# Maxima of two heads per instruction, and three PSUM banks instead of four behind ScalarE

## The chip, the cores and the metric

The kernel runs on one core of a Trainium2 chip. The metric is the device time of one execution in microseconds (us). Five engines work side by side, each with its own queue in program order: PE (TensorE, the matmuls), DVE (VectorE), ACT (ScalarE), POOL (GpSimd) and SP (SyncE, which issues DMAs). They meet only at semaphores. Matmuls write to PSUM, which has eight banks of 128 x 512 floats; another engine has to empty a bank before PE may write it again.

## The reference

For 8 sequences of 1024 tokens of width 256, a layer of attention (16 heads of width 16, rotary positions on the last 256 tokens) and a mixture of experts behind it. Cut to what matters here:

```
x = x + attention(layernorm(x))        # this change is in here
    q, k, v = xn @ wq + bq, xn @ wk, xn @ wv + bv      # 8 sequences, 16 heads, 1024 tokens, width 16
    scores = q @ k.T / 4                               # per head 1024 x 1024
    out = softmax(scores) @ v                          # softmax subtracts the row's maximum
    attention = out @ wo + bo
x = x + experts(layernorm(x))          # 16 experts, top 128 tokens each, and a shared one
```

## The kernel before

Attention works in 512 steps, 64 for each of the 8 sequences. A step V takes one group of four heads, one half of the queries (512) and one of eight tiles of 128 keys. Eight steps make a unit (one group, one half of the queries).

Scores are computed twice. **Row scores** (`score_rows`, L928): 128 queries by 512 keys of one head into one of three banks `ring`; DVE takes the row maximum of each bank (`maximum`, L630), joins the two halves of the keys once in a unit (`join_halves`, L636), and POOL writes the maxima beside the queries, so that later scores come with the maximum subtracted. The maxima run 12 steps ahead (`LEAD`), so there are twelve leading steps with nothing but row scores and a few value projections. **Turned scores** (`score_turned`, L939): 128 keys by 512 queries of one head into one of the banks `rot`; ACT takes the exponential of each (`empty`, L770). **Values** (`weigh_values`, L950): two steps later PE multiplies the exponentials with the values; all four heads of a unit add up in the bank `pv`, which ACT copies to `OT` once in a unit (`evacuate`, L824).

PE's order within a step is written out at the end of its block (L956 to L973). In this text a step reads, in PE's order:

- **A**: two row scores (heads 2 and 3); then **T0, T1**: two turned scores
- **PV**: the values of the step two before
- **B**: two row scores (heads 0 and 1); then **T2, T3**: two turned scores
- **side items** (`beside`, L108, by the table `BESIDE`): work of the sequence before or behind, none, one or two of them in a step. Projections q, k, v and the output projection are six matmuls each (L62 to L64); `xt`, `aot`, `x2t` and `ot` are transposes; `lg` are the router's logits. The transposed output `ot` stands in every eighth step (V % 8 == 3), ahead of the table's item.

What T0 to T3 and the side items write goes through the banks `rot` in turn, in PE's order (`ORDER`, L129, and `PLACE`), and ACT empties them in the same order. The item with number n waits until item n - ROT has been emptied (`bank`, L853, `rot_done`). For the row scores, `score_rows` waits in the same way on `ring_done` (L926). PE is one queue: a wait of T1 holds PV, B, T2 and T3 of its step behind it.

In the steps with V % 8 == 1, ACT's copy of `pv` to `OT` stands between the exponentials of T2 and T3 (L838). I call these **OT steps**.

After attention a second block (`feed_forward`, L984) runs the experts; the change does not touch it.

Of the kernel before, what the change touches and what calls it, by code (L numbers as in the profile page):

```python
# [4 lines left out]
F32 = mybir.dt.float32  # L5
# [7 lines left out]
AX = mybir.AxisListType  # L13

P = 128
# [51 lines left out]
def attention(nc, d, ident, SC, B):  # L67
# [9 lines left out]
    UNITS = 2 * G  # L77
    LEAD, LAG = 12, 2
    ROPE_TILES = 2
    ROT = 4  # L80
    RING = 3
    P_STEPS = 3
    LAST = B * STEPS
    CHECKS = 32 * UNITS * B
    TILES = (6, 7, 0, 1, 2, 3, 4, 5)


# [20 lines left out]
    def beside(V):  # L108

        b, S = V // STEPS, V % STEPS  # L110
        out = []
        if V >= 11 and S % 8 == 3:
            unit = (V - 11) // 8
            out.append(("ot", unit // UNITS, unit % UNITS))
        table = BESIDE if V >= 0 else FIRST
        if S in table:
            more, kind, *rest = table[S]
            if 0 <= b + more < B:
                out.append((kind, b + more, *rest))
        return out  # L120
# [16 lines left out]

    def check(m):

        unit, n = m // 32, m % 32  # L140
        return unit, (2, 3, 0, 1)[n % 4], n // 4 % 2, 4 * (unit % 2) + n // 8

    ctx = ExitStack()
    with ctx:
        def sb(name, shape, dt):
            return ctx.enter_context(nc.sbuf_tensor("sb_" + name, shape, dt))

        def sem(name):
            return ctx.enter_context(nc.semaphore(name))
# [21 lines left out]
        QT = [sb(f"QT{g}", [P, T], BF16) for g in range(G)]  # L171
        KT = [sb(f"KT{g}", [P, T], BF16) for g in range(G)]
# [8 lines left out]
        MX = sb("MX", [P, 2, 2, 4, 4], F32)  # L181
# [20 lines left out]
        total = sb("total", [P, TT], F32)  # L202
        act_scratch = sb("act_scratch", [P, 1], F32)

        ring = [ctx.enter_context(nc.psum_tensor(f"ring{i}", [P, 512], F32)) for i in range(RING)]
        rot = [ctx.enter_context(nc.psum_tensor(f"rot{i}", [P, 512], F32)) for i in range(ROT)]
        pv_bank = ctx.enter_context(nc.psum_tensor("pv", [P, 512], F32))

# [24 lines left out]
        ring_full = sem("ring_full")  # L233
        ring_done = sem("ring_done")
# [119 lines left out]
        def _(pool):  # L354
# [51 lines left out]
            def split(item, hi, lo, ready):  # L406

                _, b, h, half = item
                c = slice(512 * half, 512 * half + 512)
                pool.wait_ge(rot_done, done(item))  # L410
                own.inc(nc.gpsimd.tensor_copy(hi[:, h, c], XT[:, h, c]))
                own.wait(pool)
                nc.gpsimd.tensor_tensor(lo[:, h, c], XT[:, h, c], hi[:, h, c].bitcast(F32), ALU.subtract).then_inc(ready, 1)
# [173 lines left out]
        def _(dve):  # L587
# [38 lines left out]
            def maximum(m):  # L626

                unit, j, half, qt = check(m)
                dve.wait_ge(ring_full, m + 1)
                nc.vector.reduce_max(MX[:, unit % 2, half, j, qt % 4:qt % 4 + 1], ring[m % RING][:], AX.X  # L630
                                     ).then_inc(ring_done, 1)

            def join_halves(unit):

                dve.wait_ge(ring_done, 32 * (unit + 1))
                nc.vector.tensor_tensor(MX[:, unit % 2, 0], MX[:, unit % 2, 0], MX[:, unit % 2, 1],  # L636
                                        ALU.max).then_inc(maxima_ready, 1)

            def weighted(unit):

                dve.wait_ge(rot_done, done(("ot", unit // UNITS, unit % UNITS)))
                nc.vector.reciprocal(RD[:], AR[:, :, HD]).then_inc(recip_ready, 1)

            def top_logits(b):

                dve.wait_ge(rot_done, done(("lg", b, 3)))
                if b:
                    dve.wait_ge(shifted_ready, b)
                nc.vector.reduce_max(top[:], LG[:], AX.X).then_inc(top_ready, 1)

            def total_powers(b):

                dve.wait_ge(powers_ready, b + 1)
                if b:
                    dve.wait_ge(scored, b)
                own.inc(nc.vector.reduce_sum(total[:], powers[:], AX.X))
                own.wait(dve)
                nc.vector.reciprocal(total[:], total[:]).then_inc(total_ready, 1)
# [56 lines left out]
            for V in range(-LEAD, LAST):  # L715
                b, S = V // STEPS, V % STEPS
                prev = b > 0
                m = 4 * (V + LEAD)
                if m < CHECKS:
                    maximum(m)  # L720
                    maximum(m + 1)
                if V >= 13 and V % 8 == 5:
                    weighted((V - 13) // 8)
                if m < CHECKS:
                    maximum(m + 2)
                    maximum(m + 3)
                    if m % 32 == 28:
                        join_halves(m // 32)
                if prev and S == 52:
                    top_logits(b - 1)  # L730
                if prev and S == 56:
                    total_powers(b - 1)
# [23 lines left out]
        def _(act):  # L756
# [3 lines left out]
            def empty(item):  # L760

                n = PLACE[item]
                R = rot[n % ROT]
                kind = item[0]
# [85 lines left out]
        def _(pe):  # L850
            pe.wait_ge(ident_in, 16)

            def bank(item):  # L853

                n = PLACE[item]
                if n >= ROT:
                    pe.wait_ge(rot_done, n - ROT + 1)
                return rot[n % ROT]

# [55 lines left out]
            def head(j):  # L915

                return slice(QUAD * j, QUAD * j + QUAD)

            def score_rows(m):

                unit, j, half, qt = check(m)
                b, g = unit // UNITS, unit % UNITS // 2
                if m % 64 == 0:
                    pe.wait_ge(qk_turned[g], 32 * (b + 1))
                if m >= RING:
                    pe.wait_ge(ring_done, m - RING + 1)  # L926
                r = head(j)
                nc.tensor.matmul(ring[m % RING][:], QT[g][r, P * qt:P * qt + P], KT[g][r, 512 * half:512 * half + 512],  # L928
                                 start=True, stop=True, tile_position=(r.start, 0)).then_inc(ring_full, 1)

            def score_turned(V, j):

                unit = V // 8
                b, g, qh, kt = unit // UNITS, unit % UNITS // 2, unit % 2, V % 8
                if kt == 0 and j == 0:
                    pe.wait_ge(q2_turned[unit % 2], 16 * (unit // 2 + 1))
                R = bank(("ex", V, j))
                r = head(j)
                nc.tensor.matmul(R[:], KT[g][r, P * kt:P * kt + P], QT[g][r, 512 * qh:512 * qh + 512], start=True, stop=True,  # L939
                                 tile_position=(r.start, 0)).then_inc(rot_full, 1)  # L940

            def weigh_values(V):

                unit, kt = V // 8, V % 8
                b, g = unit // UNITS, unit % UNITS // 2
                if kt == 0 and unit:
                    pe.wait_ge(ot_ready, unit)
                pe.wait_ge(rot_done, done(("ex", V, 3)))
                for j in range(4):
                    out = nc.tensor.matmul(pv_bank[head(j), :], VA[b % 2][:, kt, 4 * g + j, :], PR[V % P_STEPS][:, j, :],  # L950
                                           start=(kt == 0), stop=(kt == TT - 1))
                out.then_inc(pv_done, 1)
# [1 line left out]
            for item in HEAD:  # L954
                fill(item)
            for V in range(-LEAD, LAST):  # L956
                m = 4 * (V + LEAD)
                if m < CHECKS:
                    score_rows(m)
                    score_rows(m + 1)  # L960
                if V >= 0:
                    for j in range(2):
                        score_turned(V, j)
                if V >= LAG:
                    weigh_values(V - LAG)
                if m < CHECKS:
                    score_rows(m + 2)
                    score_rows(m + 3)
                if V >= 0:
                    for j in range(2, 4):  # L970
                        score_turned(V, j)
                for item in beside(V):
                    fill(item)  # L973
# [596 lines left out]
def program(nc, d, B):  # L1570
    d["xn2T"] = nc.dram_tensor("xn2T", (B * D, 1024), F32, kind="Internal").ap()
    with ExitStack() as ctx:
        SC = ctx.enter_context(nc.sbuf_tensor("gate_scores", [P, 1024 // P, B * E], F32))
        ident = ctx.enter_context(nc.sbuf_tensor("identity", [P, P], F32))
        attention(nc, d, ident, SC, B)
        feed_forward(nc, d, ident, SC, B)
# [28 lines left out]
```

## Time and profile before

| | |
|---|---|
| three runs, us | 2276.67, 2281.63, 2284.34 (median 2281.63) |
| the profiled execution, us | 2277.96 |
| its span, first to last instruction, us | 2276.2 |
| PE busy, us (share of the span) | 2142.0 (94%) |
| DVE busy | 1884.7 (83%) |
| ACT busy | 1619.9 (71%) |
| POOL busy | 1207.2 (53%) |
| 2048 row maxima (L630), busy us | 1279.7 |
| 2048 exponentials (L770), busy us | 1119.5 |
| first and last turned score (L939), us from the start | 75.7 and 1402.1 |

Busy times are unions of the instructions' spans; an instruction of DVE or ACT that follows another closely begins, in the trace, before the other has ended, so that the mean of one is longer than its share of the busy time. The 1.8 us between span and execution lie before the first and behind the last instruction. Attention takes the stretch from the start to some 1430 us, the experts the rest.

### The profile page before, as it was taken

What the parts mean: (1) busy time and instruction counts of PE and PEld (TensorE: products, weight loads), DVE (VectorE), ACT (ScalarE), POOL (GpSimd) and SP (SyncE); (2) the same over time, 40 slices, a digit from 0 to 9 for tenths busy, and PEclk for the clock granted to TensorE, in tenths of its full rate; (3) what the DMA queues carried; (4) which work ended last, traced back from release to release, by engine and by line L of the source; (5) the groups of instructions that cost most, each with busy time, mean ns of one, the idle gap of its engine ahead of it and who ended that gap; (6) DMA issues with size and microseconds to landing.
All of it is one profiled execution on the core that took longest, in us unless ns stands there. A gap on an engine that the chain in (4) does not pass through costs nothing. (4 is left out here: it accounts for less than half of the span.)

```text
span 2276.2 us, 41913 instructions
## 1 busy us (share of the span) xinstructions
PE 2142.0 (94%) x15246; PEld 1232.7 (54%) x15246; DVE 1884.7 (83%) x3135; ACT 1619.9 (71%) x3092; POOL 1207.2 (53%) x1750
## 2 busy tenths in 40 slices
PE   5899999999999999999999988799999999999996
PEld 3233333333333343343343323688888888888886
DVE  6899999999999999999999994587656666666663
ACT  2599999999999999999999997333345455455451
POOL 3434576576576576586582450000024777777773
PEclk8799999999999999999999999899999999999998
DMA  4002013113103113113112111523246667667662
GB/s 118 8 24 36 18 42 73 42 39 71 54 27 81 44 39 79 36 46 70 36 43 55 36 45 40 176 83 111 83 106 144 146 120 151 146 122 149 145 123 35
DMA packets 272425, 173.03 MB, mean 76 GB/s; under 512 B 177664, under 2 KB 253312, under 8 KB 272256
## 3 DMA queue, kind: packets, MB, share of 16 engines
q1 hardware_dynamic: 247680, 137.25, 23.1%
q0 software_dynamic: 24576, 33.57, 8.4%
q8 instruction: 101, 1.65, 0.3%
q14 instruction: 68, 0.56, 0.1%
HBM read 78.50 MB, written 50.33 MB: 57 GB/s over the span
## 5 line engine op out<-in xcount | busy, mean ns | idle before, releaser
L630 DVE TENSOR_REDUCE sb_MX<-ring 128x1 f32<-128x512 f32 x2048 | 1279.7, 683 | 41.2 <-PE ring L928 19.8
L770 ACT ACTIVATE sb_PR<-rot 128x512 f32<-128x512 f32 x2048 | 1119.5, 612 | 109.0 <-PE rot L939 97.2
L928 PE MATMUL ring<-sb_KT,sb_QT 32*128 32x512 bf16 x2048 | 495.1, 392 | 66.8 <-DVE sb_MX L630 55.6
L950 PE MATMUL pv<-sb_PR,sb_VA 128*32 128x512 f32 x4096 | 547.3, 606 | 2.3 <-ACT sb_OT L824 0.6
L928 PEld LDWEIGHTS ring<-sb_KT,sb_QT 32*128 32x128 bf16 x2048 | 122.4, 91 | 652.9 <-DVE sb_MX L630 593.0
L939 PE MATMUL rot<-sb_QT,sb_KT 32*128 32x512 bf16 x2048 | 405.9, 386 | 0.9
L62 PE MATMUL ff_gu<-ff_XH,ff_WH 128*128 128x512 f32 x768 | 302.2, 394 | 14.2 <-DVE ff_XL L1367 8.7
L1312 ACT ACTIVATE ff_GL<-ff_gu 128x512 f32<-128x512 f32 x192 | 114.7, 597 | 275.1 <-PE ff_gu L64 271.5
L1383 DVE TENSOR_TENSOR ff_HF<-ff_GL,ff_gu 128x512 f32<-128x512 f32 x192 | 131.3, 686 | 209.4 <-ACT ff_GL L1312 207.8
L63 PE MATMUL ff_gu<-ff_XL,ff_WH 128*128 128x512 f32 x768 | 300.2, 391 | 0.0
L64 PE MATMUL ff_gu<-ff_XH,ff_WL 128*128 128x512 f32 x768 | 299.5, 390 | 0.0
L1261 POOL DMA_INDIRECT out<-ff_YS,ff_rows_out x128 | 214.1, 1673 | 44.0 <-issue 43.5
L1224 POOL TENSOR_TENSOR ff_pool_scratch<-identity 128x1 f32<-128x1 f32 x96 | 48.5, 505 | 352.4 <-DVE ff_taken_rows L1495 228.1
L62 PE MATMUL ff_y<-ff_WH,ff_HH 128*128 128x256 f32 x768 | 218.1, 284 | 2.9 <-DVE ff_HL L1387 2.9
L64 PE MATMUL ff_y<-ff_WH,ff_HL 128*128 128x256 f32 x768 | 218.2, 284 | 0.0
L63 PE MATMUL ff_y<-ff_WL,ff_HH 128*128 128x256 f32 x768 | 218.1, 284 | 0.0
L62 PEld LDWEIGHTS ff_gu<-ff_XH,ff_WH 128*128 128x128 f32 x768 | 144.8, 188 | 49.3 <-issue 10.8
L1244 POOL DMA_INDIRECT ff_XG<-xn,ff_rows_in x128 | 148.1, 1157 | 39.7 <-issue 39.1
L64 PEld LDWEIGHTS ff_gu<-ff_XH,ff_WL 128*128 128x128 f32 x768 | 144.6, 188 | 30.8
L63 PEld LDWEIGHTS ff_gu<-ff_XL,ff_WH 128*128 128x128 f32 x768 | 144.8, 189 | 27.6
L441 POOL TENSOR_TENSOR sb_sums<-sb_sums 128x512 f32<-128x512 f32 (+3 forms) x280 | 142.0, 507 | 19.7
L62 PEld LDWEIGHTS ff_y<-ff_WH,ff_HH 128*128 128x128 f32 x768 | 148.1, 193 | 5.1 <-DVE ff_HL L1387 3.3
(157 smaller groups left out, 3220.2 us busy)
## 6 DMA issues: line engine op xcount, KB each, us to landing
sb_XA<-x SPq DMA_DIRECT2D x8, 1024.0 KB, 5.4
sb_XR<-x SPq DMA_DIRECT2D x8, 1024.0 KB, 5.3
out<-sb_XR SPq DMA_DIRECT2D x8, 1024.0 KB, 4.5
xn<-sb_XN SPq DMA_DIRECT2D x8, 1024.0 KB, 4.5
xn2T<-sb_XT SPq DMA_DIRECT2D x8, 1024.0 KB, 4.2
ff_XG<-xn2T SPq DMA_DIRECT2D x16, 512.0 KB, 5.3
ff_X<-out SPq DMA_DIRECT2D x16, 512.0 KB, 4.6
ff_W<-WgT SPq DMA_DIRECT2D x16, 512.0 KB, 4.3
```

Of the source, the lines that this page charges most:

```text
L62: nc.tensor.matmul(out, a_hi, b_hi, start=first, stop=False)
L63: nc.tensor.matmul(out, a_hi, b_lo, start=False, stop=False)
L64: return nc.tensor.matmul(out, a_lo, b_hi, start=False, stop=last)
L441: own.inc(nc.gpsimd.tensor_tensor(to, s[:, :, 0:width], s[:, :, width:2 * width], ALU.add))
L630: nc.vector.reduce_max(MX[:, unit % 2, half, j, qt % 4:qt % 4 + 1], ring[m % RING][:], AX.X).then_inc(ring_done, 1)
L770: out = nc.scalar.activation(PR[V % P_STEPS][:, j, :], R[:], ACT.Exp, scale=0.25)
L928: nc.tensor.matmul(ring[m % RING][:], QT[g][r, P * qt:P * qt + P], KT[g][r, 512 * half:512 * half + 512], start=True, stop=True, tile_posi ...
L939: nc.tensor.matmul(R[:], KT[g][r, P * kt:P * kt + P], QT[g][r, 512 * qh:512 * qh + 512], start=True, stop=True, tile_position=(r.start, 0) ...
L950: out = nc.tensor.matmul(pv_bank[head(j), :], VA[b % 2][:, kt, 4 * g + j, :], PR[V % P_STEPS][:, j, :], start=(kt == 0), stop=(kt == TT - 1))
L1244: nc.gpsimd.indirect_dma_start(out=XG[ch.c][:, t, :], out_offset=None, in_=d["xn2"], in_offset=bass.IndirectOffsetOnAxis(ap=rows_in[:, b:b ...
L1261: nc.gpsimd.indirect_dma_start(out=d["out"], out_offset=bass.IndirectOffsetOnAxis(ap=rows_out[:, b:b + 1], axis=0), in_=YS[ch.c][:, t, :], ...
L1383: nc.vector.tensor_tensor(HF[f % 2][:], GL[f % 2][:], gu[f % 2][:, 1, 0:N], ALU.mult).then_inc(hf_ready, 1)
```

## The change

Constants: `RING` goes from 3 to 2, `ROT` from 4 to 3, and `CHECKS` (the number of maxima instructions) from 32 to 16 a unit. A `ring` is now two banks long, so PSUM is used as 2 x 2 + 3 + 1 banks instead of 3 + 4 + 1. One `score_rows` issues the two matmuls of A (or of B) into the two banks of one `ring`, with one wait ahead of the first; one `maximum` reduces both banks, 128 x 2 x 512 to 128 x 2. Both are called half as often, at the same places.

```diff
--- before.py
+++ after.py
@@ -77,11 +77,11 @@
     UNITS = 2 * G
     LEAD, LAG = 12, 2
     ROPE_TILES = 2
-    ROT = 4
-    RING = 3
+    ROT = 3
+    RING = 2
     P_STEPS = 3
     LAST = B * STEPS
-    CHECKS = 32 * UNITS * B
+    CHECKS = 16 * UNITS * B
     TILES = (6, 7, 0, 1, 2, 3, 4, 5)
 
 
@@ -137,8 +137,8 @@
 
     def check(m):
 
-        unit, n = m // 32, m % 32
-        return unit, (2, 3, 0, 1)[n % 4], n // 4 % 2, 4 * (unit % 2) + n // 8
+        unit, n = m // 16, m % 16
+        return unit, (2, 0)[n % 2], n // 2 % 2, 4 * (unit % 2) + n // 4
 
     ctx = ExitStack()
     with ctx:
@@ -202,7 +202,7 @@
         total = sb("total", [P, TT], F32)
         act_scratch = sb("act_scratch", [P, 1], F32)
 
-        ring = [ctx.enter_context(nc.psum_tensor(f"ring{i}", [P, 512], F32)) for i in range(RING)]
+        ring = [ctx.enter_context(nc.psum_tensor(f"ring{i}", [P, 2, 512], F32)) for i in range(RING)]
         rot = [ctx.enter_context(nc.psum_tensor(f"rot{i}", [P, 512], F32)) for i in range(ROT)]
         pv_bank = ctx.enter_context(nc.psum_tensor("pv", [P, 512], F32))
 
@@ -626,13 +626,13 @@
             def maximum(m):
 
                 unit, j, half, qt = check(m)
-                dve.wait_ge(ring_full, m + 1)
-                nc.vector.reduce_max(MX[:, unit % 2, half, j, qt % 4:qt % 4 + 1], ring[m % RING][:], AX.X
+                dve.wait_ge(ring_full, 2 * m + 2)
+                nc.vector.reduce_max(MX[:, unit % 2, half, j:j + 2, qt % 4], ring[m % RING][:], AX.X
                                      ).then_inc(ring_done, 1)
 
             def join_halves(unit):
 
-                dve.wait_ge(ring_done, 32 * (unit + 1))
+                dve.wait_ge(ring_done, 16 * (unit + 1))
                 nc.vector.tensor_tensor(MX[:, unit % 2, 0], MX[:, unit % 2, 0], MX[:, unit % 2, 1],
                                         ALU.max).then_inc(maxima_ready, 1)
 
@@ -715,17 +715,15 @@
             for V in range(-LEAD, LAST):
                 b, S = V // STEPS, V % STEPS
                 prev = b > 0
-                m = 4 * (V + LEAD)
+                m = 2 * (V + LEAD)
                 if m < CHECKS:
                     maximum(m)
-                    maximum(m + 1)
                 if V >= 13 and V % 8 == 5:
                     weighted((V - 13) // 8)
                 if m < CHECKS:
-                    maximum(m + 2)
-                    maximum(m + 3)
-                    if m % 32 == 28:
-                        join_halves(m // 32)
+                    maximum(m + 1)
+                    if m % 16 == 14:
+                        join_halves(m // 16)
                 if prev and S == 52:
                     top_logits(b - 1)
                 if prev and S == 56:
@@ -920,13 +918,14 @@
 
                 unit, j, half, qt = check(m)
                 b, g = unit // UNITS, unit % UNITS // 2
-                if m % 64 == 0:
+                if m % 32 == 0:
                     pe.wait_ge(qk_turned[g], 32 * (b + 1))
                 if m >= RING:
                     pe.wait_ge(ring_done, m - RING + 1)
-                r = head(j)
-                nc.tensor.matmul(ring[m % RING][:], QT[g][r, P * qt:P * qt + P], KT[g][r, 512 * half:512 * half + 512],
-                                 start=True, stop=True, tile_position=(r.start, 0)).then_inc(ring_full, 1)
+                for n in range(2):
+                    r = head(j + n)
+                    nc.tensor.matmul(ring[m % RING][:, n, :], QT[g][r, P * qt:P * qt + P], KT[g][r, 512 * half:512 * half + 512],
+                                     start=True, stop=True, tile_position=(r.start, 0)).then_inc(ring_full, 1)
 
             def score_turned(V, j):
 
@@ -954,18 +953,16 @@
             for item in HEAD:
                 fill(item)
             for V in range(-LEAD, LAST):
-                m = 4 * (V + LEAD)
+                m = 2 * (V + LEAD)
                 if m < CHECKS:
                     score_rows(m)
-                    score_rows(m + 1)
                 if V >= 0:
                     for j in range(2):
                         score_turned(V, j)
                 if V >= LAG:
                     weigh_values(V - LAG)
                 if m < CHECKS:
-                    score_rows(m + 2)
-                    score_rows(m + 3)
+                    score_rows(m + 1)
                 if V >= 0:
                     for j in range(2, 4):
                         score_turned(V, j)
```

The rows below are of ACT, in a step with one side item (`KP`, a key projection) and the OT step behind it, in the first sequence; `PR` are the exponentials, the number behind `rot` is the bank. First before, then now:

```order
L770 ACTIVATE sb_PR1<-rot0 128x512 [waits pv_done,rot_full]
L770 ACTIVATE sb_PR1<-rot1 128x512 [waits rot_full]
L770 ACTIVATE sb_PR1<-rot2 128x512 [waits rot_full]
L770 ACTIVATE sb_PR1<-rot3 128x512 [waits rot_full]
L794 CAST sb_KP<-rot0 128x4x4x16 [waits rot_full]
L770 ACTIVATE sb_PR2<-rot1 128x512 [waits pv_done,rot_full]
L770 ACTIVATE sb_PR2<-rot2 128x512 [waits rot_full]
L770 ACTIVATE sb_PR2<-rot3 128x512 [waits rot_full]
L824 COPY sb_OT<-pv 128x512 [waits pv_done]
L770 ACTIVATE sb_PR2<-rot0 128x512 [waits rot_full]
```

```order
L768 ACTIVATE sb_PR1<-rot2 128x512 [waits pv_done,rot_full]
L768 ACTIVATE sb_PR1<-rot0 128x512 [waits rot_full]
L768 ACTIVATE sb_PR1<-rot1 128x512 [waits rot_full]
L768 ACTIVATE sb_PR1<-rot2 128x512 [waits rot_full]
L792 CAST sb_KP<-rot0 128x4x4x16 [waits rot_full]
L768 ACTIVATE sb_PR2<-rot1 128x512 [waits pv_done,rot_full]
L768 ACTIVATE sb_PR2<-rot2 128x512 [waits rot_full]
L768 ACTIVATE sb_PR2<-rot0 128x512 [waits rot_full]
L822 COPY sb_OT<-pv 128x512 [waits pv_done]
L768 ACTIVATE sb_PR2<-rot1 128x512 [waits rot_full]
```

The order is the same. The banks come round after three: in the second piece T2 and T3 of the first step are in rot1 and rot2, the side item in rot0, and T0 and T1 of the next step again in rot1 and rot2; in the first piece T1 of the next step (rot2) is in the bank of T2, one further back.

PE in two steps without a side item, from B of the first to PV of the second; `ring` are row scores, `rot` turned scores, `pv` the values. First before, then now:

```order
L928 MATMUL ring1<-sb_KT3,sb_QT3 128x512 [waits ring_done]
L928 MATMUL ring2<-sb_KT3,sb_QT3 128x512 [waits ring_done]
L939 MATMUL rot3<-sb_QT2,sb_KT2 128x512 [waits rot_done]
L939 MATMUL rot0<-sb_QT2,sb_KT2 128x512 [waits rot_done]
L928 MATMUL ring0<-sb_KT3,sb_QT3 128x512 [waits ring_done]
L928 MATMUL ring1<-sb_KT3,sb_QT3 128x512 [waits ring_done]
L939 MATMUL rot1<-sb_QT2,sb_KT2 128x512 [waits rot_done]
L939 MATMUL rot2<-sb_QT2,sb_KT2 128x512 [waits rot_done]
L950 MATMUL pv<-sb_PR1,sb_VA0 32x512 [waits rot_done,ot_ready]
```

```order
L927 MATMUL ring1<-sb_KT3,sb_QT3 128x512 [waits ring_done]
L927 MATMUL ring1<-sb_KT3,sb_QT3 128x512
L938 MATMUL rot0<-sb_QT2,sb_KT2 128x512 [waits rot_done]
L938 MATMUL rot1<-sb_QT2,sb_KT2 128x512 [waits rot_done]
L927 MATMUL ring0<-sb_KT3,sb_QT3 128x512 [waits ring_done]
L927 MATMUL ring0<-sb_KT3,sb_QT3 128x512
L938 MATMUL rot2<-sb_QT2,sb_KT2 128x512 [waits rot_done]
L938 MATMUL rot0<-sb_QT2,sb_KT2 128x512 [waits rot_done]
L949 MATMUL pv<-sb_PR1,sb_VA0 32x512 [waits rot_done,ot_ready]
```

The matmuls stand in the same order. The second of each pair of row scores has lost its wait; its first now waits for a whole double bank. T1 of the second step is in the bank of T2 (rot0) now, and was in the bank of T1 before that.

## Rows read from the trace of the kernel before

**Rows 1.** Windows: busy us and count of each engine, granted clock, DMA share, GB/s.

```profile
400.00:800.00 400.00, 385.26 (x3168) 149.33 (x3166) 391.10 (x659) 370.39 (x769) 256.93 (x434) 1.00 0.20 51
...
1390.00:1400.00 10.00, 9.16 (x61) 2.21 (x61) 0.25 (x1) 9.97 (x21) 0.62 (x1) 1.00 0.01 2
```

**Rows 2.** The page's groups: count, busy us, mean ns, idle before and releaser.

```profile
L630 DVE TENSOR_REDUCE sb_MX<-ring 128x1 f32<-128x512 f32 x2048 | 1279.7, 683 | 41.2 <-PE ring L928 19.8
```

**Rows 3.** Line L939, the turned scores: ns min/median/max, first and last start.

```profile
L939 PE MATMUL rot<-sb_QT,sb_KT x2048: 370/385/605, 75.7 to 1402.1; 32*128 32x512 bf16 x187
```

**Rows 4.** Timeline, step without side item: start us, length, engine, line, [idle before].

```profile
907.42 0.39 PE L939 MATMUL rot<-sb_QT,sb_KT 32*128 32x512 bf16 x2
...
907.84 0.69 DVE L630 TENSOR_REDUCE sb_MX<-ring 128x1 f32<-128x512 f32 x1
...
908.58 0.38 PE L928 MATMUL ring<-sb_KT,sb_QT 32*128 32x512 bf16 x1 [0.31 <-DVE sb_MX L630]
...
909.91 0.39 PE L939 MATMUL rot<-sb_QT,sb_KT 32*128 32x512 bf16 x2
```

**Rows 5.** Timeline of PE, a step with one projection beside it.

```profile
776.84 0.39 PE L939 MATMUL rot<-sb_QT,sb_KT 32*128 32x512 bf16 x2
777.16 0.38 PE L62 MATMUL rot<-sb_WH,sb_AH 128*128 128x256 f32 x1
...
778.07 0.39 PE L939 MATMUL rot<-sb_QT,sb_KT 32*128 32x512 bf16 x2
...
779.40 0.39 PE L939 MATMUL rot<-sb_QT,sb_KT 32*128 32x512 bf16 x2
```

**Rows 6.** Timeline of PE, T2 of the step with two side items.

```profile
773.90 0.39 PE L939 MATMUL rot<-sb_QT,sb_KT 32*128 32x512 bf16 x2
```

**Rows 7.** Timeline, the last maxima: one step in which T1 waits for ACT.

```profile
1376.97 0.39 PE L939 MATMUL rot<-sb_QT,sb_KT 32*128 32x512 bf16 x2
...
1377.45 0.60 ACT L770 ACTIVATE sb_PR<-rot 128x512 f32<-128x512 f32 x1 [0.24 <-PE rot L939]
...
1377.95 0.59 ACT L770 ACTIVATE sb_PR<-rot 128x512 f32<-128x512 f32 x1
...
1378.11 0.38 PE L939 MATMUL rot<-sb_QT,sb_KT 32*128 32x512 bf16 x1
1378.42 0.64 PE L950 MATMUL pv<-sb_PR,sb_VA 128*32 128x512 f32 x4
...
1379.42 0.39 PE L939 MATMUL rot<-sb_QT,sb_KT 32*128 32x512 bf16 x3
```

**Rows 8.** Timeline, an OT step with one projection: PE's T2, ACT's copy, next T2.

```profile
768.72 0.39 PE L939 MATMUL rot<-sb_QT,sb_KT 32*128 32x512 bf16 x2
...
769.20 0.60 ACT L770 ACTIVATE sb_PR<-rot 128x512 f32<-128x512 f32 x1
...
770.16 0.62 ACT L770 ACTIVATE sb_PR<-rot 128x512 f32<-128x512 f32 x1
...
771.33 0.39 PE L939 MATMUL rot<-sb_QT,sb_KT 32*128 32x512 bf16 x2
```

**Rows 9.** Timeline of PE, the 89th us: the fifth step's T0 and T1.

```profile
88.71 0.39 PE L939 MATMUL rot<-sb_QT,sb_KT 32*128 32x512 bf16 x2
```

**Rows 10.** DVE: eight maxima in a row, and the short maxima of L649.

```profile
46.61 4.88 DVE L630 TENSOR_REDUCE sb_MX<-ring 128x1 f32<-128x512 f32 x8 [1.02 <-PE ring L928]
...
L649 DVE TENSOR_REDUCE sb_top<-sb_LG x8: 274/276/286, 381.8 to 1430.7; 128x8 f32<-128x128 f32 x8
```

**Rows 11.** Timeline of PE, a leading step with one projection, and the next's start.

```profile
42.47 0.61 PE L928 MATMUL ring<-sb_KT,sb_QT 32*128 32x512 bf16 x3
43.86 0.60 PE L928 MATMUL ring<-sb_KT,sb_QT 32*128 32x512 bf16 x1 [0.78 <-DVE sb_MX L630]
44.39 0.58 PE L62 MATMUL rot<-sb_WH,sb_XH 128*128 128x256 f32 x1
...
45.97 0.61 PE L928 MATMUL ring<-sb_KT,sb_QT 32*128 32x512 bf16 x3
```

## The prediction

> **What bounds the kernel now.** I read the windows first, then the groups of the page, then single steps in the timeline.
>
> The windows [rows 1] say that between 400 and 800 us everything is busy: DVE 391.10 of 400 us, PE 385.26, ACT 370.39. The groups put 1279.7 us of DVE on the 2048 maxima, with 41.2 us idle before them [rows 2]. From this DVE looks like the bound. The steps say otherwise; attention is 512 of them, 1402.1 - 75.7 = 1326.4 us from the first T0 to the last T3, 2.59 us each [rows 3]. I measure a step from T2 to the next T2.
>
> A step with no side item takes 909.91 - 907.42 = 2.49 us [rows 4]. The reduction that starts at 907.84 ends at 908.53, the second matmul of A follows at 908.58, and PE had stood idle for 0.31 us: T0, T1, PV and B are all held by one wait for DVE. So here DVE and PE's in-order queue together set the pace.
>
> A step with one projection takes 779.40 - 776.84 = 2.56 us [rows 5], and PE sets it: from 777.16 to 778.07 it does the projection, then everything follows. One with two items takes 776.84 - 773.90 = 2.94 us [rows 5, 6]. A faster DVE gives such steps nothing. 42 steps have two items; 211 have one projection or logits, 84 one transpose of the table, 21 `ot` alone; 153 have none. (Counted from the table and the rule for `ot`, with sequences that have no neighbour on one side left out; 511 intervals between 512 steps.)
>
> **The loop through ACT.** The trace shows what PE does where T1 has to wait for ACT, once at the end of the maxima, with one side item in the step [rows 7]. T2 and T3 issue at 1376.97; the exponential of T2 runs from 1377.45 to 1378.05; T1 of the next step, which needs T2's bank because ROT is 4, issues at 1378.11; PV at 1378.42; the next T2 at 1379.42. So the loop is 0.48 + 0.60 + 0.06 + 0.31 + 1.00 = 2.45 us from T2 to T2. The second exponential, of T3, ends at 1377.95 + 0.59 = 1378.54, or 0.49 later.
>
> **The change part by part.** ROT from 4 to 3. T1 comes five items behind T0 of the step before if there is no side item, six with one, seven with two. Three back from it is then T2, T3 or the first side item; before it was T1, T2 or T3. The order of ACT shows it: behind a step with one item, T1 is in the bank of T3. By step:
>
> - None: T1 waits for T2: the loop of 2.45 us. It was 2.49 here, so the old wait for DVE goes and the wait for ACT comes in its place.
> - One item: T1 waits for T3: 2.45 + 0.49 = 2.94 us, with a projection, a transpose or logits alike, since all of them lie in PE's wait. T1 would be ready 0.32 + 0.91 = 1.23 us after T2 [rows 5] and has to wait until 0.48 + 0.60 + 0.49 + 0.06 = 1.63: PE stands idle for 0.40 us.
> - One item in an OT step: the copy to `OT` lies between the two exponentials. T3's starts at 770.16 against 769.20 for T2's, and takes 0.62, so it ends 0.98 instead of 0.49 later [rows 8]. 2.45 + 0.98 = 3.43 us, against 771.33 - 768.72 = 2.61 now.
> - No item in an OT step: T1 needs T2 only, and PV waits for the copy as now: 2.61 us.
> - Two items: the second waits for T2, until 0.48 + 0.60 + 0.06 = 1.14, then takes 0.91, then A, T0, T1 (0.01), 0.31 and 1.00: 3.37 us, against 2.94. (T1's own wait, for the copy of `ot`, ends earlier.)
>
> The sum of the 511 intervals: without item 139 x 2.45 = 340.6 (130, and 9 at the end where no maxima are left); OT without item 14 x 2.61 = 36.5; one item 267 x 2.94 = 785.0 (162 projections, 63 transposes, 21 logits, and `ot` alone 21); OT with item 49 x 3.43 = 168.1; two items 42 x 3.37 = 141.5. Together 1471.7 us. The four opening steps run at the low clock and take 88.71 - 75.7 = 13.0 us [rows 9] where these figures have 10.3, so 2.7 more: 1474.4. That is 148 us more than 1326.4.
>
> The maxima. Eight in a row take 4.88 us [rows 10], so one follows another after (4.88 - 0.68) / 7 = 0.60 us. A reduction of 1024 elements does not occur. From 276 ns for 128 elements [rows 10] to 683 for 512 [rows 2] is 1.06 ns an element, so 1024 would take 1.23 us, and two together 2.3 to 2.5 us a step. The lower end is 1.06 (twice the 0.60 less the 0.14 that this line leaves at zero elements), the upper end two whole ones, 1.37. I take 1.23, the line through both rows. At each of them the cost is nothing: twice 1.37 is 2.74, under the 2.94 of most steps. Only steps without item would feel the upper end, by 2.74 - 2.45. What hides it is the wait for ACT; the saving of 0.07 to 0.3 us a step lies in the same shade and gives nothing.
>
> Two double banks. A fills both banks of one `ring` once DVE is done with its last A. In a step of 2.94 us with A 1.23 behind B, DVE starts A 1.65 behind T2 (0.42 from matmul to reduction, as 907.42 to 907.84), ends at 2.9, and the next A on PE is due at 4.2. In a step of 2.45, the last A ends at about 0.3 and T1 cannot issue before 1.14. So `ring_done` is not the wait that ends last, in spite of one buffer less. The wait that goes on the second matmul of each pair is worth nothing by itself.
>
> The twelve leading steps have no turned scores. With a projection one takes 45.97 - 42.47 = 3.50 us, because three banks hold less than a step: the third maximum is done before PE continues [rows 11]. With two double banks, B can follow A while the projection is pending; PE's part is 1.58 (44.39 to 45.97) and twice the 0.53 from 43.86 to 44.39: 2.64. Seven such steps save 6 us; the other five save little. I take 6 (bounds 0 and 10). The head and the tail of attention pass through three banks as well: 1 us more. POOL and SP get more time per step; nothing of theirs is late. The experts are as before.
>
> 148 - 6 + 1 = 143 us. The profiled execution took 2277.96, so 2421; the median of the three runs lies 3.7 above it: **2425 us**.
>
> **The rivals.** *DVE's relief decides* (faster). The maxima are the largest group, on the busiest engine, and two in one save 0.60 + 0.68 - 1.23 = 0.05 us or at most 0.14 (1.37 - 1.23). If T1's waits cost nothing, the 258 steps that PE does not set (153, 84 and 21) would gain twice that, some 0.1 to 0.28 us each, or 26 to 72 us, and the lead 6: about 2230. Against it: PE cannot pass T1, and rows 7 show it waiting there with four banks. The Trainium skill, Perfetto Trace Analysis, section Optimizing Scalar/DVE Operations, says that grouping into larger operations helps if the engine is saturated, and gives about 125 ns per operation on PSUM; by it an estimate of 1024 x 0.125 = 128 us would come off DVE. The trace agrees that DVE is nearly saturated and not that its time ends steps.
>
> *The waits are half hidden*: ACT gets T2 and T3 earlier than I think, so that only OT steps and those with two items lose: 49 x 0.82 + 42 x 0.43 = 58, less 6 and less 139 x 0.04: 2328. Nothing in rows 4 or 7 speaks for it.
>
> *The reduction of two banks is the bound*: above 1.47 us each it passes 2.94 / 2; at 1.6 us all 511 steps take 3.2 or more, +165 over the forecast or so, 2590. The line through two rows speaks against it.
>
> *The clock falls* with PE idle for 0.4 us of 2.94: at half speed the 0.31 and 1.00 of each loop double, 511 x 1.31 = +670, about 3090. But the granted clock stayed at 1.00 (2.4 GHz) between 1390 and 1400 us [rows 1], where PE also waits for ACT in each step. The same page of the Trainium skill, section Matmul Optimizations, says that PE's power follows its utilization and asks for back-to-back matmuls. The trace shows the full clock at this much idling.
>
> **How the numbers follow.** Forecast 0.83; relief 0.04; half hidden 0.06; reduction 0.03; clock 0.02; no net change, some of each, 0.02. Anything within 0.3% (7 us) would be no measurable change. Slower is all but the relief and the last: 0.94; same 0.02; faster 0.04. For the range: each loop is read to 0.01 or 0.02 us, times 511 steps is 10 us; the upper end of the reduction adds 139 x 0.29 = 40 in steps without item, and ends there; if transposes beside steps hide part of the wait, 84 x 0.3 = 25 goes. I take 2390 to 2455.
>
> **What would show it.** Idle time of PE before T1 (L938 after) released by ACT's exponentials, about 0.40 us in each step with one item, and T1 0.06 us behind T3's exponential. Steps of 2.94 us with one projection, 3.43 in OT steps, 3.37 with two items. DVE with a maximum of 1.2 us and long waits for PE's row scores; ACT waiting longer for turned scores. PE's waits for `ring_done` nearly gone. I am wrong if one-item steps stay near 2.56, or if PE's wait there is for DVE.

## The result and the profile after

The changed kernel takes 2435.47 us (median; 2426.68 to 2438.14) against 2279.25 for the kernel before on the same chip: 1.0673 times, 95% interval 1.0656 to 1.0691. It is slower by 156 us. The forecast was 2425, within 2390 to 2455. The profiled execution took 2435.52, with a span of 2433.7.

The first lines that answer to those of before are the groups of the page, DVE, ACT, PE's turned scores and PE's row scores (count, busy us, mean ns, idle before with its releaser; lines moved by two or less):

```profile
L630 DVE TENSOR_REDUCE sb_MX<-ring 128x2 f32<-128x1024 f32 x1024 | 1231.4, 1223 | 228.9 <-PE ring L927 208.9
L768 ACT ACTIVATE sb_PR<-rot 128x512 f32<-128x512 f32 x2048 | 1112.0, 606 | 256.7 <-PE rot L938 254.9
L938 PE MATMUL rot<-sb_QT,sb_KT 32*128 32x512 bf16 x2048 | 562.3, 390 | 97.6 <-ACT sb_PR L768 89.3
L927 PE MATMUL ring<-sb_KT,sb_QT 32*128 32x512 bf16 x2048 | 389.8, 391 | 16.4 <-DVE sb_MX L630 10.6
```

Half as many maxima take 1223 ns each, and DVE is less busy (1231.4 us against 1279.7 in [rows 2]). But its idle time has gone from 41.2 to 228.9 us, 208.9 of it for row scores that come late from PE. ACT waits for PE as well. PE is the one that waits for ACT: DVE and ACT starve behind one queue.

The view of the line L938, PE's row and what the engine's idle time ahead of it ended with (weight loads included):

```profile
L938 PE MATMUL rot<-sb_QT,sb_KT x2048: 371/385/629, 69.1 to 1558.2; 32*128 32x512 bf16 x187
...
  ACT sb_PR L768: 350.6, 667
```

The turned scores now take from 69.1 to 1558.2, or 1489.1 us, where [rows 3] have 1326.4: 162.7 more in the 511 steps, and they start 6.6 earlier. That is the result; from the last turned score to the end of the span it is 875.5 us, before it was 874.1, so the experts take what they took. The same view of before has 17.5 us in 40 waits.

One step with one projection, by the timeline (as in [rows 5]; the last rows of ACT and PE are narrower windows, so that two instructions show apart):

```profile
847.90 0.39 PE L938 MATMUL rot<-sb_QT,sb_KT 32*128 32x512 bf16 x2
848.22 0.39 PE L62 MATMUL rot<-sb_WH,sb_AH 128*128 128x256 f32 x1
...
849.14 0.39 PE L927 MATMUL ring<-sb_KT,sb_QT 32*128 32x512 bf16 x2
...
849.84 1.07 PE L949 MATMUL pv<-sb_PR,sb_VA 128*32 128x512 f32 x8
...
850.85 0.39 PE L938 MATMUL rot<-sb_QT,sb_KT 32*128 32x512 bf16 x2
...
848.39 0.60 ACT L768 ACTIVATE sb_PR<-rot 128x512 f32<-128x512 f32 x1 [0.24 <-PE rot L938]
...
848.88 0.59 ACT L768 ACTIVATE sb_PR<-rot 128x512 f32<-128x512 f32 x1
...
849.53 0.39 PE L938 MATMUL rot<-sb_QT,sb_KT 32*128 32x512 bf16 x1
```

T2 and T3 issue at 847.90, their exponentials start at 848.39 and 848.88. PE has done the projection, A and T0 by 849.14, 1.24 us after T2. T1 issues at 849.53, 0.06 behind the end of T3's exponential (849.47), and only then PV (849.84) and the next T2 (850.85). The step takes 2.95 us instead of 2.56, and the 0.39 is T1's wait.

The OT step of the same unit (as in [rows 8]):

```profile
838.16 0.39 PE L938 MATMUL rot<-sb_QT,sb_KT 32*128 32x512 bf16 x2
...
839.14 0.58 ACT L822 COPY sb_OT<-pv 128x512 f32<-128x512 f32 x1
...
839.60 0.62 ACT L768 ACTIVATE sb_PR<-rot 128x512 f32<-128x512 f32 x1
...
840.27 0.39 PE L938 MATMUL rot<-sb_QT,sb_KT 32*128 32x512 bf16 x1 [0.49 <-ACT sb_PR L768]
...
841.59 0.39 PE L938 MATMUL rot<-sb_QT,sb_KT 32*128 32x512 bf16 x2
```

The copy lies between the two exponentials, T3's ends at 840.22, T1 follows at 840.27, and the step takes 3.43 us.

The windows, in the middle of attention and in its last steps (as in [rows 1]):

```profile
400.00:800.00 400.00, 373.35 (x2836) 140.63 (x2829) 336.11 (x317) 331.08 (x686) 238.75 (x400) 1.00 0.17 43
...
1530.00:1540.00 10.00, 8.53 (x36) 1.12 (x35) 0.00 (x0) 5.60 (x12) 0.00 (x0) 0.50 0.01 2
```

In the middle the granted clock is 1.00 as before. At the end, where before had 1.00 between 1390 and 1400, it is 0.50. That was not in the forecast, and is the largest part of the result that the prediction's sum does not hold.

### The profile page after: what moved, and what is told of

It is laid out like the page before. It is cut to its first block and busy times, and to the rows that moved or that the text cites. A ratio compares the mean times of both kernels' runs of the same rounds, so it can differ in the third digit from the quotient of the medians.

```text
span 2433.7 us, 40890 instructions
## 1 busy us (share of the span) xinstructions
PE 2248.4 (92%) x15246; PEld 1253.4 (52%) x15246; DVE 1835.8 (75%) x2111; ACT 1621.8 (67%) x3092; POOL 1207.2 (50%) x1750
## 5 line engine op out<-in xcount | busy, mean ns | idle before, releaser
L630 DVE TENSOR_REDUCE sb_MX<-ring 128x2 f32<-128x1024 f32 x1024 | 1231.4, 1223 | 228.9 <-PE ring L927 208.9
L938 PE MATMUL rot<-sb_QT,sb_KT 32*128 32x512 bf16 x2048 | 562.3, 390 | 97.6 <-ACT sb_PR L768 89.3
L949 PE MATMUL pv<-sb_PR,sb_VA 128*32 128x512 f32 x4096 | 556.4, 616 | 1.2
L927 PE MATMUL ring<-sb_KT,sb_QT 32*128 32x512 bf16 x2048 | 389.8, 391 | 16.4 <-DVE sb_MX L630 10.6
L927 PEld LDWEIGHTS ring<-sb_KT,sb_QT 32*128 32x128 bf16 x2048 | 92.6, 91 | 514.5 <-DVE sb_MX L630 373.3
L938 PEld LDWEIGHTS rot<-sb_QT,sb_KT 32*128 32x128 bf16 x2048 | 134.4, 91 | 278.9 <-ACT sb_PR L768 261.4
```

The costliest lines, as they stand in the source:

```text
L630: nc.vector.reduce_max(MX[:, unit % 2, half, j:j + 2, qt % 4], ring[m % RING][:], AX.X).then_inc(ring_done, 1)
L927: nc.tensor.matmul(ring[m % RING][:, n, :], QT[g][r, P * qt:P * qt + P], KT[g][r, 512 * half:512 * half + 512], start=True, stop=True, til ...
```

## The experiments

The theory: all of the loss is ROT = 3, by T1's wait for the exponential of T3, and nothing in the row scores or maxima matters, except in the lead. The rivals: the double banks or the merged maxima cost or save something; ACT's total load sets the pace; the clock. Each ratio below is to the kernel before on the same chip, where its median was between 2279 and 2283 us.

**Three banks alone.** The kernel before, with one number changed.

```diff
-    ROT = 4
+    ROT = 3
```

> The kernel before with ROT = 3 and nothing else: single banks, one maximum each. Loop theory (T1 waits for the exponential of T3 behind every side item): one-item steps 2.94 us, OT steps with an item 3.43, two items 3.37, steps without item stay at the 2.49 that DVE sets; 2279 + 148 + 139 x 0.04 + 1, and 0 to 12 more if the granted clock falls in the last steps: 2433 to 2446 us. Rival (the double banks and the merged maxima make it slower, the three banks are harmless): about 2279.

Measured: 2445.91 us (2443.62 to 2448.18), 1.0716 times before (1.0696 to 1.0735). The same step with one projection, PE's T2, PV and next T2, and T1 from a narrower window:

```profile
858.55 0.39 PE L939 MATMUL rot<-sb_QT,sb_KT 32*128 32x512 bf16 x2
...
860.49 1.07 PE L950 MATMUL pv<-sb_PR,sb_VA 128*32 128x512 f32 x8
...
861.49 0.39 PE L939 MATMUL rot<-sb_QT,sb_KT 32*128 32x512 bf16 x2
...
860.17 0.39 PE L939 MATMUL rot<-sb_QT,sb_KT 32*128 32x512 bf16 x1
```

2.94 us, T1 1.62 behind T2, with single banks and single maxima. One constant brings the whole loss, and 10 us more than the whole change; so the rest of the change saves about 10. Of these, 6.6 are the lead (the first turned score is at 75.7 here and at 69.1 in the changed kernel); in steps without item this kernel keeps the 2.49 us that it had, where the changed one has 2.455, over 130 steps 5 us more.

**Two maxima on a double bank.** The changed kernel, with the merged instruction taken apart again. (`ring_done` counts once for each 512 columns then, and the waits on it are doubled to match.)

```diff
-                dve.wait_ge(ring_full, 2 * m + 2)
-                nc.vector.reduce_max(MX[:, unit % 2, half, j:j + 2, qt % 4], ring[m % RING][:], AX.X
-                                     ).then_inc(ring_done, 1)
+                for n in range(2):
+                    dve.wait_ge(ring_full, 2 * m + n + 1)
+                    nc.vector.reduce_max(MX[:, unit % 2, half, j + n, qt % 4:qt % 4 + 1], ring[m % RING][:, n, :], AX.X
+                                         ).then_inc(ring_done, 1)
```

> The changed kernel, but each double bank is reduced by two maxima of 512 elements instead of one of 1024. Loop theory: neither direction matters, the maxima lie in the shade of ACT's loop: 2435 us, within 6. Rival that DVE's time decides and the merged maximum saves: 0.05 to 0.14 us a pair, 1024 pairs, 50 to 140 us slower than 2435. Rival that the maximum over two banks is what costs: back towards 2279.

Measured: 2437.98 us (2434.47 to 2439.99), 1.0687 times before (1.0668 to 1.0706). That interval overlaps with the changed kernel's. DVE's group on its page:

```profile
L631 DVE TENSOR_REDUCE sb_MX<-ring 128x1 f32<-128x512 f32 x2048 | 1281.9, 684 | 179.5 <-PE ring L928 175.5
```

The 50 us by which DVE is busier than in the changed kernel are what its idle time has lost. The merged maximum is worth nothing that these runs can tell; the 2.455 us of a step without item and the early lead (the first turned score is at 69.9) are there without it, and come from the double banks.

**One more copy on ACT, ahead of T3's exponential, or behind it.** The same instruction in both, once in each of the 512 steps; the second variant has the two lines behind the exponential's `then_inc`. The copy's result is read by nobody.

```diff
+                if kind == "ex" and item[2] == 3:
+                    nc.scalar.copy(act_more[:], ident[:])
                 act.wait_ge(rot_full, n + 1)
```

> The changed kernel with one more copy of 128 x 128 on ACT in each step, between the exponentials of T2 and T3. Loop theory: it delays T3's exponential by 0.15 to 0.2 us, and with it T1 behind every step with an item; 316 such steps, so 47 to 63 us more, 2482 to 2498; one-item steps 3.1 us, steps without item stay at 2.45. Rival (ACT has slack of 0.6 us in a step of 2.94, so 0.2 us more is hidden): 2435.

> The same copy, directly behind T3's exponential instead of ahead of it. Loop theory: ACT has as much more to do as in the run before, but T1 does not wait for it; only the 42 steps with two items wait for the item behind it, some 0.1 us each: 2435 to 2441; one-item steps stay at 2.94. Rival (ACT's total time decides): as slow as with the copy ahead of it, 2482 to 2498.

Measured: ahead of it 2508.20 us (2506.33 to 2512.18), 1.0997 times before (1.0976 to 1.1019); behind it 2434.13 (2430.41 to 2441.29), 1.0678 times (1.0652 to 1.0703). Ahead of it, the step with one projection reads:

```profile
881.03 0.39 PE L941 MATMUL rot<-sb_QT,sb_KT 32*128 32x512 bf16 x2
...
882.01 0.29 ACT L765 COPY sb_act_more<-identity 128x128 f32<-128x128 f32 x1
...
882.20 0.60 ACT L771 ACTIVATE sb_PR<-rot 128x512 f32<-128x512 f32 x1
...
882.86 0.38 PE L941 MATMUL rot<-sb_QT,sb_KT 32*128 32x512 bf16 x1 [0.20 <-ACT sb_PR L771]
...
884.18 0.39 PE L941 MATMUL rot<-sb_QT,sb_KT 32*128 32x512 bf16 x2
```

Behind it:

```profile
850.46 0.39 PE L941 MATMUL rot<-sb_QT,sb_KT 32*128 32x512 bf16 x2
...
853.40 0.39 PE L941 MATMUL rot<-sb_QT,sb_KT 32*128 32x512 bf16 x2
...
851.44 0.59 ACT L769 ACTIVATE sb_PR<-rot 128x512 f32<-128x512 f32 x1
851.91 0.30 ACT L820 COPY sb_act_more<-identity 128x128 f32<-128x128 f32 x1
...
852.09 0.39 PE L941 MATMUL rot<-sb_QT,sb_KT 32*128 32x512 bf16 x1
```

The copy costs 0.20 us of ACT. Ahead of T3's exponential the step takes 3.15 us, and T1 follows that exponential as before; behind it the step stays at 2.94. So the same load is free in one place and costs 73 us in the other. It is the place between T2 and T3 that PE waits for, not the total of ACT. Of the 73, 316 steps with one item at 0.20 make 62 to 63, and two items 42 x 0.05 another 2. The rest, 8, is more than I expected, and takes the time 10 us past the end of the expected range. In this run's trace the granted clock fell twice in the middle (last section), for three steps each, which lengthened them by 2.4 and 2.1 us; the fall at the end of attention began four steps earlier than in the changed kernel and ended three steps before the last, which is some 1.7 us more.

**PE kept busy in the last steps.** The changed kernel; behind T3 of the twelve steps in which no maxima are left, three row scores that nobody reads (`keep_busy`, 32 x 128 by 32 x 512 into the first bank of the first `ring`).

```diff
+                if m >= CHECKS:
+                    if m == CHECKS:
+                        pe.wait_ge(ring_done, CHECKS)
+                    keep_busy(3)
```

> The changed kernel; in the last twelve steps, where no maxima are left, PE gets three more row scores behind T3 that nobody reads, 0.2 us each, in the time in which it waits for T1. If the clock fell there because PE idled, it stays at 1.00 and the steps take 2.45 instead of 3.69 us: 12 us less than the changed kernel, 2423. Rival (the clock falls at this place for another reason): 3.69 or more, 2435.

Measured: 2421.88 us (2419.71 to 2428.57), 1.0626 times before (1.0607 to 1.0645), so 13.6 below the changed kernel by the medians and 0.0047 by the ratios, whose intervals do not overlap. Two rows answer each other. The changed kernel, a step without item at the end, T2 with T0 of the next, T1, PV, T2:

```profile
1535.59 0.61 PE L938 MATMUL rot<-sb_QT,sb_KT 32*128 32x512 bf16 x3
1536.89 0.60 PE L938 MATMUL rot<-sb_QT,sb_KT 32*128 32x512 bf16 x1 [0.68 <-ACT sb_PR L768]
1537.42 1.94 PE L949 MATMUL pv<-sb_PR,sb_VA 128*32 128x512 f32 x8
1539.29 0.61 PE L938 MATMUL rot<-sb_QT,sb_KT 32*128 32x512 bf16 x3
```

And with the three row scores (T2, the extra matmuls, T0 and T1, PV, T2), and the window around it:

```profile
1531.36 0.39 PE L938 MATMUL rot<-sb_QT,sb_KT 32*128 32x512 bf16 x2
1531.37 0.82 PE L958 MATMUL ring<-sb_KT,sb_QT 32*128 32x512 bf16 x3
1532.03 0.79 PE L938 MATMUL rot<-sb_QT,sb_KT 32*128 32x512 bf16 x2
1532.75 1.06 PE L949 MATMUL pv<-sb_PR,sb_VA 128*32 128x512 f32 x8
1533.75 0.39 PE L938 MATMUL rot<-sb_QT,sb_KT 32*128 32x512 bf16 x2
```

```profile
1520.00:1540.00 20.00, 19.66 (x126) 4.80 (x124) 0.74 (x3) 17.82 (x37) 1.03 (x2) 1.00 0.12 49
```

3.70 us at a granted clock of 0.50 (1.2 GHz) without, 2.39 at 1.00 (2.4 GHz) with more work. Without them PE idled for 0.5 to 0.7 us of each step, the clock fell, and each step got longer by it; in the profiled execution with the idle time filled it did not fall. One trace does not decide this, since among the other kernels the fall at the end differs from trace to trace (last section). What speaks for it is the time of all runs, by a narrow gap: the 95% interval of the ratio ends at 1.0645 with the row scores and begins at 1.0656 without.

**Four banks in the lead, nothing else.** The kernel before, with single banks and four `rot`; in the twelve leading steps row scores also go into the bank `pv`, which is idle until the third step (`AHEAD` is 4 x `LEAD`). DVE's maxima take the same bank, and the first PV waits until the leading maxima are done.

```diff
+        def ring_bank(m):
+            return (ring + [pv_bank])[m % 4] if m < AHEAD else ring[m % RING]
...
-                    pe.wait_ge(ring_done, m - RING + 1)
+                    pe.wait_ge(ring_done, m - (3 if m < AHEAD else RING - 1))
```

> The kernel before (single banks, ROT = 4, RING = 3), but in the twelve leading steps, before any values are weighed, the row scores also use the idle bank pv, four in turn. If the lead gained from four row-score banks instead of three and not from the merged maxima, the first turned score comes at 69 to 70 us instead of 75.7, and the kernel takes 2273, 6 less than before. Rival (the merged maxima gave it): the first turned score stays at 75.7 and the time at 2279.

Measured: 2273.39 us (2271.79 to 2277.01, nine runs), 0.9969 times before (0.9957 to 0.9980). Its turned scores:

```profile
L944 PE MATMUL rot<-sb_QT,sb_KT x2048: 371/384/604, 70.4 to 1396.6; 32*128 32x512 bf16 x187
```

The first one is 5.3 us earlier, the last 5.5. So most of the lead's gain of 6.6 us is that of a fourth row-score bank and needs no merged maximum. This part of the change can be had without giving up a bank `rot`, and the kernel is then 0.3% faster than the kernel before.

## Why the prediction was right

By its steps, with the medians of T2 to T2 over all steps of each kind in the trace after:

| kind of step (intervals) | forecast, us | measured, us |
|---|---|---|
| no item (130) | 2.45 | 2.455 |
| OT, no item (13) | 2.61 | 2.615 |
| one projection / transpose / logits / `ot` alone (266) | 2.94 | 2.944 / 2.944 / 2.943 / 2.943 |
| OT and one item (49) | 3.43 | 3.433 |
| two items (42) | 3.37 | 3.366 |
| no item, at the end (9) | 2.45 | 3.69 (2.39 to 3.69) |

*The loop through ACT* was right to a hundredth of a microsecond, and shown by three banks alone and by the copy ahead of and behind T3's exponential. *The reduction of 1024 elements* was 1.223 us, forecast 1.23, and hidden as forecast. That the size came out so close is in part luck: the row at 128 elements through which the line was drawn [rows 10] is a reduction of `sb_LG`, in SBUF, to eight results, and not of a PSUM bank to one. *The double banks'* wait did not end last: the page has 10.6 us of waits of PE's row scores L927 for DVE, 8.2 of them in the first 90 us. *The lead* saved 6.6 us, forecast 6.

What was too small is one term, the sum of the intervals: 1474.4 forecast, 1489.1 measured. The last eleven intervals, from the 501st step on, account for 11.8 of these 14.7: forecast 9 x 2.45 + 2.61 + 2.94 = 27.6, measured 39.4. Of the remaining 2.9, 1.0 lies between the first T0 and the first T2, which the forecast's sum of intervals does not hold, and the rest is spread over the other 500 intervals. So the clock rival came true there, at the price that it had been given (3.69 - 2.39 = 1.30 us a step, forecast 1.31), after I had set it aside on a row of before. That row does not show "this much idling": ACT paced those steps at 1.96 us, and PE was idle for 0.84 of 10 us [rows 1], where in the changed kernel it idles for 0.53 of 2.39 before T1 alone. In the middle of attention, where I had meant it, the clock stayed at 1.00.

The headline is closer than the sum. The sum gave 2421 for the profiled execution, which took 2435.5; the 3.7 us that the forecast added, from profiled execution to median, did not recur (2435.52 and 2435.47), and by luck hid as much of the miss. The upper end of the range does not follow from its own terms either: 2425 and 40 for the reduction are 2465, and 2455 was taken. The result lies inside by either.

*DVE's relief* failed: behind the lead, row scores waited for DVE for 2.5 us in all, and the experiment with two maxima shows its 50 us to be without effect. The Trainium skill, Perfetto Trace Analysis, section Optimizing Scalar/DVE Operations, says that larger operations can help "if the engine is saturated". Here the same edit ended that: between 400 and 800 us DVE went from 391.10 us busy to 336.11.

## What to carry to other kernels

Count how many fills lie between a fill and the one that reuses its bank, in the steps with the most fills and not on average: one bank fewer moved the wait from T2's exponential to T3's, and a matmul in front of an in-order queue held everything behind it. Two engines at 96% and 98% (between 400 and 800 us before) say little about which of them sets the pace; a step written out in the timeline, from an instruction to its repetition, gives the loop, and a change can be priced from its terms. And before a bank is taken from one rotation for another, ask which of the two waits is the last: here the fourth row-score bank gained some 5 us in the steps without item and 5 to 7 in the lead, and the lost bank behind ACT, by itself, cost 164, the fall of the clock at the end included.

## What was not expected of the hardware

The granted clock can fall where PE has been waiting in each step, and a fall then lengthens the steps by more than the wait. In the changed kernel it fell to 0.50 at about 1522 us, after little more than two steps without row scores, in which PE idled before T1 for about 0.5 us in 2.4:

```profile
1521.26 0.54 PE L938 MATMUL rot<-sb_QT,sb_KT 32*128 32x512 bf16 x3
1522.33 0.39 PE L938 MATMUL rot<-sb_QT,sb_KT 32*128 32x512 bf16 x1 [0.53 <-ACT sb_PR L768]
```

In the run with the copy ahead of T3's exponential it also fell in the middle, in steps with logits, in two of the sequences (window of that run):

```profile
1000.00:1006.00 6.00, 6.00 (x33) 2.55 (x30) 2.56 (x3) 2.63 (x7) 0.00 (x0) 0.50 0.01 3
```

There three steps each time took 3.6 to 4.8 us instead of 3.1 to 3.6, and the clock came back. In steps of 2.455 us without item, in the middle of the changed kernel, it did not fall, though PE waits for T1 there too; what tells the two apart was not tried.

Nor does the same waiting bring the fall each time. In the run with the copy behind T3's exponential, PE issues the last steps as in the changed kernel, T1 1.07 us behind T2 in both, and yet the clock stayed at 1.00 from the start of these steps to 1538 us and then fell for 3.4 us only; nine of its last eleven intervals took 2.39 us, or 2.55 in the OT step (T2, T3 and T0, then T1, then a window of that run):

```profile
1531.94 0.73 PE L941 MATMUL rot<-sb_QT,sb_KT 32*128 32x512 bf16 x3
1533.01 0.39 PE L941 MATMUL rot<-sb_QT,sb_KT 32*128 32x512 bf16 x1 [0.34 <-ACT sb_PR L769]
```

```profile
1522.00:1536.00 14.00, 11.73 (x76) 2.63 (x72) 0.49 (x2) 13.14 (x30) 2.01 (x6) 1.00 0.24 84
```

In the run with two maxima it fell and came back to 1.00 for the last three intervals, with the waits unchanged. So PE's waits alone do not settle when the clock falls; what does, these runs do not show. The spread among runs of one kernel may come from the fall at the end: of the changed kernel's four runs three had a mean clock of 0.973 or 0.974 and took 2435 to 2438 us, and one had 0.981 and took 2426.7. That is a correlation of four runs, not a test.
